# A third group of nodes summed from gathered rows: three of 25 groups in 13 rounds, in place of two in 9

## The chip, the cores and the metric

The kernel runs on one core of one Trainium2 chip. The metric is the device time of one execution in microseconds; where several executions are timed, the median stands for them.

## What is computed

One layer of a graph network on 6250 nodes with 206250 edges, 128 features each, all float32. The edges come sorted by their target node `dst`; `src` is in no order.

```python
def _L0_gnn_ref(node_features, edge_features, src, dst, W_node, b_node, W_edge, b_edge, W_msg, b_msg):
    h = node_features @ W_node.T + b_node
    e = edge_features @ W_edge.T + b_edge
    msg = h[src] + e
    msg = msg @ W_msg.T + b_msg
    n = node_features.shape[0]
    s = jax.ops.segment_sum(msg, dst, num_segments=n)
    deg = jax.ops.segment_sum(jnp.ones(dst.shape, msg.dtype), dst, num_segments=n)
    return s / jnp.maximum(deg, 1.0)[:, None]

x = _layernorm(x + _L0_gnn_ref(x, edge_attr_128, src, dst, ...), axis=-1)
```

## The kernel before

The two products with weights are taken out of the sum over edges: a node needs the sum of the edge features that point at it, the sum of the rows `x[src]` of those edges, and its number of edges. The nodes are cut into 25 groups of 250 (`NB`).

**Edge features.** The edges are cut into 101 blocks of 2048. SP loads a block of 1 MB (line 483) into one of three buffers `edges`; a buffer is free when PE has read the block that was there (`l1_done`). DVE builds a one-hot table (`onehot`, line 923) and a placing table (`place`, line 929). PE sums the block into 32-wide windows with 16 matmuls a quarter of the array wide (line 691), ACT copies them (line 1448), PE places them in 144 columns (line 698) and DVE adds these to `sums_e` (line 944).

**Rows of x, by counts.** For most groups the sum of `x[src]` is made as a product: a matrix of counts (how often node j is a source of target i) by x. A round does this for one group. POOL loads the group's pieces of `src` (`load_window`, line 604); DVE makes keys and then five pairs of one-hot tables `row_hot` and `key_hot` (`make_hots`, line 954), one pair for each of the round's five segments. PE makes the counts in 25 fills of five matmuls, five fills a segment (`count_fill`, line 802); ACT moves each fill out of PSUM (`move_bank`, lines 1539 to 1547); PE multiplies the counts by x in 98 matmuls (`apply_counts`, line 814), spread over the second half of the round and the first of the next. Before there are 23 rounds.

**Rows of x, gathered.** For the remaining `GX` groups, 2 before, the rows are fetched. The first `XBLOCKS` edge blocks, 9, cover the edges of these groups. For each of the 2048 edges of such a block POOL gathers the row `x[src]` into `x_gathered`, by 16 indirect DMAs of 128 rows (`load_rows`, line 625), and PE sums the block a second time with these rows in place of the edge features (line 691 with `x_gathered`), with the same tables, into columns of `sums_e` set aside for it (`X_COLS`, `X_LONG`).

There is one buffer `x_gathered`. The first gather of block k waits until PE has used block k−1, and each gather waits for a fill of the rounds:

```python
room = (x_round[k] - x_round[k - 1] if k > 0 else 2) * ROUND_FILLS
x_fill.append([x_round[k] * ROUND_FILLS + XSEG * FILLS - room + 2 + (room - 9) * i // (TILES - 1) for i in range(TILES)])
...
if k > 0:
    pool.wait_ge(l1_done, last_item[sup_of.index(k - 1)] + 1)
pool.wait_ge(bank_filled, x_fill[k][i])
```

PE uses a gathered block at the start of the round's fourth segment (`XSEG` = 3), behind fill 15 of 25, once all 16 DMAs have landed (`rows_in`). `x_round` says which rounds have one: before 5, 6, 8, 10, 12, 13, 15, 17 and 19. The gathers and the window loads share POOL in the order of their fills (`pool_loads`); a round's window load stands at fill 10. The other edge blocks are taken in pairs, in the third and the fifth segment of each round.

**Finishing.** When a group's sums are whole, PE multiplies them by the weights (`finish_group`, lines 826 and, for a gathered group, 829) into the bank `misc_ps`, which must be free of the group finished before; DVE adds message, bias and residual and takes the statistics, ACT normalises, SP stores. The group of round m is finished in the first segment of round m+2. A gathered group is finished once the blocks that hold it are summed (`X_DONE`).

Of the kernel before, what the change touches and what calls it, by code (L numbers as in the profile page):

```python
# [31 lines left out]
SEGS = 5  # L32
# [10 lines left out]
EDGE_SLOTS = 3  # L43
ONEHOT_SLOTS = 3
COUNT_BANKS = 3
GX = 2
XBLOCKS = 9
X_COLS = 2000
X_LONG = 700
BLOCK = 128  # L50
JOBS = 2
NEAR = 3
# [5 lines left out]
def gnn_layer(nc, x, src, dst, edge_attr, w_node, b_node, w_edge, b_edge, w_msg, b_msg, out):  # L58
# [5 lines left out]
    GROUPS = N // NB  # L64
    ROUNDS = GROUPS - GX
    B_ROUNDS = GROUPS - G0
# [9 lines left out]
    def area_of(b):  # L76
        return max(0, STEP * b - AHEAD)
# [5 lines left out]
    JOB_DVE = (13, 4)  # L83
    JOB_ROWS = (B_ROUNDS - NEAR, G0 - GX)
    JOB_ROUND = (NEAR, B_ROUNDS)
# [13 lines left out]
    SLOTS_B, SLOTS_A, DEGREES = 9, 17, 13  # L99
    group_of = [G0 + m if m < B_ROUNDS else GX + m - B_ROUNDS for m in range(ROUNDS)]  # L100
    XSEG = 3
    x_round = [5 + 14 * k // (XBLOCKS - 1) for k in range(XBLOCKS)]
    x_slot = [LEAD + SEGS * m + XSEG for m in x_round]
    ordered = [FIRST + i if FIRST + i < NS else FIRST + i - NS + XBLOCKS for i in range(NS - XBLOCKS)]
    PAIRS = -(-(NS - XBLOCKS - LEAD) // 2)
    sup_of, blocks_at, ordered_by, items_by, item_of = [], [], [0], [0], []
    for u in range(SLOTS):
        m, s = divmod(u - LEAD, SEGS)
        pairs = -(-PAIRS * (2 * m + (s >= 2) + (s >= 4)) // (2 * ROUNDS))
        due = u + 1 if u < LEAD else min(NS - XBLOCKS, LEAD + 2 * pairs)  # L110
        blocks_at.append(list(range(len(sup_of), len(sup_of) + due - ordered_by[-1])))
# [3 lines left out]
        if u in x_slot:  # L115
            assert not blocks_at[u]
            k = x_slot.index(u)
# [8 lines left out]
    slot_of = [next(u for u in range(SLOTS) if t in blocks_at[u]) for t in range(NS)]  # L126
    assert x_round[-1] < B_ROUNDS + 2 and sorted(sup_of) == list(range(NS)) and max(len(ts) for ts in blocks_at) <= 2 and ITEMS == NS + XBLOCKS


    X_DONE = [5, 9]  # L130
    ordered_x = {u: sum(len(blocks_at[w]) for w in range(u)) for u in range(SLOTS + 1)}
    finishes = [(LEAD + SEGS * (m + 2) + (3 if m == 0 else 0) if m < ROUNDS - 2 else SLOTS, m, None) for m in range(ROUNDS)]
    for i in range(GX):
        u = x_slot[X_DONE[i] - 1] + SEGS
        finishes.append((u if u not in x_slot else u + SEGS, None, i))
    finishes.sort(key=lambda f: f[0])
    finish_slot = [f[0] for f in finishes]
    finish_of = {m: n for n, (u, m, i) in enumerate(finishes) if m is not None}
# [3 lines left out]

    ZERO_FIN = 1 + max(n for n, g in enumerate(finished) if g * NB < X_COLS + X_LONG and (g + 1) * NB > X_COLS)
    ZERO_X = finish_slot[ZERO_FIN - 1] + 1
    assert ZERO_X < x_slot[0] and X_COLS >= N0 + AREA and area_of(XBLOCKS - 1) + AREA <= X_LONG and area_of(SCRATCH_SAFE - 1) + AREA <= SCRATCH

# [3 lines left out]
    for u, m, i in finishes:  # L150
# [3 lines left out]
        if m is None:  # L154
            assert LIMIT_X[0] + LIMIT_X[1] * (2 * i + 1) <= X_DONE[i]
        elif m < B_ROUNDS:
# [15 lines left out]
    with ExitStack() as ctx:  # L172
        def sb(name, shape, dt=F32):
            return ctx.enter_context(nc.sbuf_tensor(name, shape, dt))
# [92 lines left out]
        deg_rows = rows_words[0:CHUNKS, JOBS * (NB + 2) + PB + 1:JOBS * (NB + 2) + 2 * PB + 1]  # L267
        limit_x = sb("limit_x", [2 * GX, 1])
        limit = [sb(f"limit{k}", [JOB_ROWS[k], 1]) for k in range(JOBS)]
# [640 lines left out]
        def _(dve):  # L910
# [249 lines left out]
            def make_degrees():  # L1160
                dve.wait_ge(chunk_rows_in, 32)
                dve.tensor_scalar(check_junk[0:2 * GX, 16:17], chunk_rows[0:2 * GX, PB:PB + 1], limit_x[:, 0:1], None, ALU.is_gt, ALU.add,
                                  accum_out=viol[0:2 * GX, 13:14])
# [274 lines left out]
        def _(act):  # L1438
# [135 lines left out]
            for u in range(SLOTS):  # L1574
# [3 lines left out]
                if u == ZERO_X:  # L1578
                    act.wait_ge(fin_mm, ZERO_FIN)
                    act.copy(sums_e[:, X_COLS:X_COLS + X_LONG], zero_col[:, 0:1].to_broadcast([P, X_LONG])).then_inc(zeroed, 1)  # L1580
                if u < LEAD:
# [84 lines left out]
```

## Time and profile before

| | us |
|---|---|
| median of 3 runs | 718.48 (717.97 to 718.91) |
| the profiled execution | 714.08 |
| span in its profile | 712.2 |
| PE busy | 647.9 |
| DVE busy | 591.8 |
| ACT busy | 460.3 |
| POOL busy | 234.6 |

The span is the time from the first to the last recorded instruction of the profiled execution; 1.9 us lie outside it. PE is the matmul engine, PEld its weight loads, DVE the vector engine, ACT the scalar engine, POOL the one that issues the gathers, SP the one that issues plain loads and stores. "Busy" is time in which an engine has an instruction in work. In a timeline row the first number is the start in us from the span's start, the second the time that the row covers, and the brackets tell the idle time ahead of it and what ended that.

### The profile page before, as it was taken

The numbers are of one execution on the slowest core, as the hardware profiler recorded it, in microseconds if no ns is written. First come the engines' busy times: TensorE is split into PE (matmuls) and PEld (weight loads), VectorE is DVE, ScalarE is ACT, GpSimd is POOL, SyncE is SP. The second block draws the span as 40 slices with busy tenths as digits, with TensorE's granted clock in tenths as the row PEclk, the third lists the DMA queues.
The fourth block names the chain that finished last, engine by engine and source line by source line (L and its number), as shares of the span: only waits on it lengthen the run. The fifth ranks groups of instructions, "written<-read, shape, count | busy, mean of one in ns | idle before, by whom it ended". The sixth has DMA issues, their size and how long they took to land.

```text
span 712.2 us, 22423 instructions
## 1 busy us (share of the span) xinstructions
PE 647.9 (91%) x9313; PEld 592.6 (83%) x9313; DVE 591.8 (83%) x1156; ACT 460.3 (65%) x954; POOL 234.6 (33%) x199
## 2 busy tenths in 40 slices
PE   2699977989999979999999999799999999999994
PEld 2577866878989969999999889798899999989994
DVE  7685697869999868998989899598899898898873
ACT  3147798637657646766767666476677676676772
POOL 3212000210534755434435548354255255000000
PEclk9999999979999999999999999999999999999998
DMA  6881524534556764765865466665755865853400
GB/s 201 288 254 40 168 98 136 186 120 167 185 180 209 254 223 145 263 198 170 279 199 165 153 216 206 213 207 180 233 207 195 260 195 181 274 174 135 143 15 18
DMA packets 81507, 130.55 MB, mean 183 GB/s; under 512 B 12100, under 2 KB 25126, under 8 KB 81303
## 3 DMA queue, kind: packets, MB, share of 16 engines
q1 hardware_dynamic: 73230, 115.79, 48.7%
q0 software_dynamic: 7200, 12.39, 6.2%
q8 instruction: 77, 1.26, 0.7%
q10 hardware_dynamic: 974, 0.90, 0.5%
q14 instruction: 26, 0.21, 0.1%
HBM read 125.80 MB, written 3.23 MB: 181 GB/s over the span
## 4 chain that ended last, share of the span: by engine, by line
PE 75%; DVE 11%; issue 4%; ACT 4%; DMA 3%; POOL 2%; ACTq 0%; DVEq 0%; POOLq 0%
PE x_ps L814 36%; PE count_ps L802 16%; PE win_ps L691 13%; PE win_ps L698 3%; DVE key_hot L954 3%; DVE row_hot L954 2%; PE misc_ps L826 2%; POOL x_gathered L625 1%; DMA x_gathered<-in_x_dram,x_index 1%; PE x_ps L737 1%; DVE x_gathered L1075 1%; PE count_ps L737 1%; ACT counts L1539 1%; DMA win_src<-in_src_dram,clipped_int 1%; PE x_ps L721 1%
## 5 line engine op out<-in xcount | busy, mean ns | idle before, releaser
L814 PE MATMUL x_ps<-x_parts,counts 128*125 128x256 f32 x2254 | 391.2, 301 | 6.5 <-ACT counts L1544 6.5
L1547 ACT CAST counts<-count_ps 128x490 fp32r<-128x490 f32 x552 | 321.9, 604 | 105.3 <-PE count_ps L802 102.5
L814 PEld LDWEIGHTS x_ps<-x_parts,counts 128*125 128x125 f32 x2254 | 299.6, 189 | 9.8 <-ACT counts L1544 9.8
L625 POOL DMA_INDIRECT x_gathered<-in_x_dram,x_index x144 | 186.6, 1296 | 243.8 <-PE count_ps L802 231.0
L954 DVE TENSOR_TENSOR row_hot<-iota_bf,row 125x3200 bf16<-125x3200 bf16 x115 | 209.6, 1822 | 50.9 <-PE count_ps L802 29.3
L802 PE MATMUL count_ps<-key_hot,row_hot 125*128 125x98 bf16 x2875 | 216.5, 209 | 12.8 <-ACT counts L1547 9.4
L802 PEld LDWEIGHTS count_ps<-key_hot,row_hot 125*128 125x128 bf16 x2875 | 149.2, 98 | 44.1 <-issue 11.3
L954 DVE TENSOR_TENSOR key_hot<-iota_bf,key 125x2500 bf16<-125x2500 bf16 x115 | 167.2, 1454 | 0.0
L691 PE MATMUL win_ps<-edges,onehot 128*32 128x128 f32 x3232 | 104.6, 282 | 0.2 <-DVE sums_e L944 0.2
L691 PEld LDWEIGHTS win_ps<-edges,onehot 128*32 128x32 f32 x3232 | 88.1, 113 | 9.1 <-issue 1.4
L1448 ACT COPY win_sb<-win_ps 128x128 f32<-128x128 f32 x110 | 29.0, 267 | 72.5 <-PE win_ps L691 70.8
L604 POOL DMA_INDIRECT win_src<-in_src_dram,clipped_int x23 | 34.3, 1490 | 82.3 <-DVEq L1122 65.0
L944 DVE TENSOR_TENSOR sums_e<-sums_e,win_ps 128x144 f32<-128x144 f32 x110 | 33.0, 300 | 26.7 <-PE win_ps L698 25.3
L923 DVE TENSOR_TENSOR onehot<-iota_bf,rel_col 128x352 f32<-128x352 bf16 x101 | 48.0, 510 | 0.0
L698 PE MATMUL win_ps<-place,win_sb 128*128 128x144 f32 x220 | 37.2, 290 | 1.6 <-ACT win_sb L1448 1.6
L698 PEld LDWEIGHTS win_ps<-place,win_sb 128*128 128x128 f32 x220 | 31.1, 191 | 2.3 <-ACT win_sb L1448 2.2
L929 DVE TENSOR_SCALAR place<-iota_f,pos 128x144 f32<-128x144 f32 x101 | 30.3, 300 | 0.2
L1566 ACT ACTIVATE y<-y,shift,rstd 125x128 f32<-125x128 f32 x50 | 22.4, 509 | 3.6 <-DVE shift L1041 3.6
L653 PE MATMUL x_ps<-ones_bf,region 101*125 101x1 bf16 x48 | 5.5, 245 | 15.4 <-DVE region L1046 15.4
L1539 ACT CAST counts<-count_ps 128x245 fp32r<-128x245 f32 x23 | 9.0, 391 | 15.3 <-PE count_ps L802 15.3
L653 PEld LDWEIGHTS x_ps<-ones_bf,region 101*125 101x125 bf16 x48 | 5.3, 227 | 16.1 <-DVE region L1046 10.8
L826 PE MATMUL misc_ps<-w_both,sums_e 128*125 128x128 f32 x100 | 16.1, 282 | 2.7 <-issue 2.7
(214 smaller groups left out, 417.2 us busy)
## 6 DMA issues: line engine op xcount, KB each, us to landing
edges<-in_edge_attr_dram SPq DMA_DIRECT2D x101, 1024.0 KB, 6.8
resid<-in_x_dram SPq DMA_DIRECT2D x25, 125.0 KB
out_dram<-y SPq DMA_DIRECT2D x25, 125.0 KB
x_gathered<-in_x_dram,x_index POOLq DMA_INDIRECT x144
region<-in_dst_dram ACTq DMA_DIRECT2D x1, 768.0 KB
win_src<-in_src_dram,clipped_int POOLq DMA_INDIRECT x23, 3.6
x_index<-in_src_dram SPq DMA_DIRECT2D x9, 8.0 KB, 5.8
region<-in_L_gnn_W_node_dram SPq DMA_DIRECT2D x1, 64.0 KB
```

The lines of the kernel that those rows point to most:

```text
L604: pool.indirect_dma_start(out=win_src[:, m % 3, :], out_offset=None, in_=src.rearrange("(r e) -> r e", e=WE), in_offset=bass.IndirectOffse ...
L625: pool.indirect_dma_start(out=x_gathered[:, i, :], out_offset=None, in_=x[:, :], in_offset=bass.IndirectOffsetOnAxis(ap=x_index[:, k, i:i ...
L691: mm = pe.matmul(bank[q * W:(q + 1) * W, 0:D], hot[:, q * J + j, :], rows, start=(j == 0), stop=(j == J - 1))
L698: pe.matmul(l2_ps[v % 2], win_sb[:, v % 2, :], place[:, t % 2, :], start=True, stop=True).then_inc(l2_done, 1)
L802: mm = pe.matmul(fill_bank(fill)[:, k * KEYS:(k + 1) * KEYS], row_hot[0:WE, g % 2, f * FILL + k, :], key_hot[0:WE, g % 2, f * FILL + k, 0: ...
L814: mm = pe.matmul(x_ps[m % 2][0:PB, h * 2 * D:(h + 1) * 2 * D], counts[h][:, b, :], x_parts[:, b, :, :].rearrange("p k d -> p (k d)"), star ...
L826: mm = pe.matmul(to, sums_e[:, first + h * PB:first + (h + 1) * PB], w_both[:, 1, :], start=True, stop=(i is None))
L923: dve.tensor_tensor(onehot[:, t % ONEHOT_SLOTS, :, 0:SPAN], iota_bf[:, 0:SPAN].rearrange("p (a w) -> p a w", a=1).to_broadcast([P, TILES, ...
L929: dve.tensor_scalar(place[:, t % 2, :], iota_area[:, :], pos[:, sup_of[t]:sup_of[t] + 1], None, ALU.is_equal).then_inc(place_ready, 1)
L944: dve.tensor_tensor(to, to, l2_ps[v % 2], ALU.add).then_inc(added, 1)
L954: ins = dve.tensor_tensor(hot[0:WE, g % 2, :, :].rearrange("p w (a b) -> p w a b", b=4), iota_bf[0:WE, 0:width].rearrange("p (c a b) -> p ...
L1547: ins = act.copy(counts[h][:, :, at - h * PB:at - h * PB + FILL * 2], nodes)
```

## The change

`GX` goes from 2 to 3 and `XBLOCKS` from 9 to 13. With one group more gathered there are 22 rounds in place of 23. The gathered blocks stand in the rounds 7 to 19, one in each, in place of every second round or so from 5 to 19. The set-aside columns grow from 700 to 950. A gathered group is finished three segments after the segment of its last block, in the second segment of the next round, in place of five or ten after it.

```diff
-GX = 2
-XBLOCKS = 9
+GX = 3
+XBLOCKS = 13
 X_COLS = 2000
-X_LONG = 700
+X_LONG = 950
...
     XSEG = 3
-    x_round = [5 + 14 * k // (XBLOCKS - 1) for k in range(XBLOCKS)]
+    x_round = [7 + k for k in range(XBLOCKS)]
     x_slot = [LEAD + SEGS * m + XSEG for m in x_round]
...
-    X_DONE = [5, 9]
+    X_DONE = [5, 9, 13]
...
     for i in range(GX):
-        u = x_slot[X_DONE[i] - 1] + SEGS
-        finishes.append((u if u not in x_slot else u + SEGS, None, i))
+        finishes.append((x_slot[X_DONE[i] - 1] + SEGS - 2, None, i))
```

The changed file is one line shorter, so that a line behind the diff has a number less by one there.

POOL's program, from the first gathered blocks on. In the kernel before (`win_src` is the window load of a round, `x_gathered` a gather, with how many stand in a row):

```order
L604 DMA win_src<-in_src_dram,clipped_int 125x125 x4
L625 DMA x_gathered<-in_x_dram,x_index 128x128 x7
L604 DMA win_src<-in_src_dram,clipped_int 125x125
L625 DMA x_gathered<-in_x_dram,x_index 128x128 x9
L604 DMA win_src<-in_src_dram,clipped_int 125x125
L625 DMA x_gathered<-in_x_dram,x_index 128x128 x16
L604 DMA win_src<-in_src_dram,clipped_int 125x125
L625 DMA x_gathered<-in_x_dram,x_index 128x128 x7
L604 DMA win_src<-in_src_dram,clipped_int 125x125
L625 DMA x_gathered<-in_x_dram,x_index 128x128 x9
```

The same place in the changed kernel:

```order
L603 DMA win_src<-in_src_dram,clipped_int 125x125 x6
L624 DMA x_gathered<-in_x_dram,x_index 128x128 x7
L603 DMA win_src<-in_src_dram,clipped_int 125x125
L624 DMA x_gathered<-in_x_dram,x_index 128x128 x9
L603 DMA win_src<-in_src_dram,clipped_int 125x125
L624 DMA x_gathered<-in_x_dram,x_index 128x128 x16
L603 DMA win_src<-in_src_dram,clipped_int 125x125
L624 DMA x_gathered<-in_x_dram,x_index 128x128 x16
```

A block with a round between it and the one before has its 16 gathers split by a window load, 7 and 9; a block in the next round has all 16 between two window loads. Before there are two such blocks, now twelve, all but the first.

PE's program around the finish of the first gathered group. Before, in the fourth segment of round 14 (`turn_keys` is lines 786 and 787, then the four matmuls of the finish):

```order
L786 MATMUL misc_ps<-ident_bf,row_bf 125x125
L787 MATMUL misc_ps<-ident_bf,key_bf 125x125
L802 MATMUL count_ps<-key_hot,row_hot 128x98 x5
L814 MATMUL x_ps<-x_parts,counts_49 125x256 x5
L826 MATMUL misc_ps<-w_both,sums_e 125x128
L829 MATMUL misc_ps<-w_both,sums_e 125x128
L826 MATMUL misc_ps<-w_both,sums_e 125x128
L829 MATMUL misc_ps<-w_both,sums_e 125x128
```

In the changed kernel, in the second segment of round 12 and the start of the third (`edges` at the end is the pair of blocks there):

```order
L801 MATMUL count_ps<-key_hot,row_hot 128x98 x5
L813 MATMUL x_ps<-x_parts,counts_50 125x256 x4
L825 MATMUL misc_ps<-w_both,sums_e 125x128
L828 MATMUL misc_ps<-w_both,sums_e 125x128
L825 MATMUL misc_ps<-w_both,sums_e 125x128
L828 MATMUL misc_ps<-w_both,sums_e 125x128
L801 MATMUL count_ps<-key_hot,row_hot 128x98 x5
L813 MATMUL x_ps<-x_parts,counts_50 125x256 x5
L690 MATMUL win_ps<-edges,onehot 32x128 x32
```

The finish of the gathered group now stands ahead of the round's first pair of blocks, five fills behind the finish of the group that is finished in that round's first segment. With three of them, they fall in rounds 12, 16 and 20; before in 14 and 20.

## Rows read from the trace of the kernel before

**Rows 1.** The page: span, busy time and share of engines; index load.
```profile
span 712.2 us, 22423 instructions
PE 647.9 (91%) x9313; PEld 592.6 (83%) x9313; DVE 591.8 (83%) x1156; ACT 460.3 (65%) x954; POOL 234.6 (33%) x199
...
x_index<-in_src_dram SPq DMA_DIRECT2D x9, 8.0 KB, 5.8
```
**Rows 2.** Windows by round: rounds 6, 7, 8, 13, 20, 22; 5 to 22 together.
```profile
243.71:276.61 32.90, 28.70 (x438) 26.34 (x435) 24.15 (x43) 18.40 (x38) 17.71 (x14) 0.95 0.61 199
276.61:301.41 24.80, 24.49 (x370) 22.88 (x367) 22.78 (x39) 17.65 (x36) 14.21 (x11) 1.00 0.61 209
301.41:328.68 27.27, 26.96 (x438) 25.06 (x435) 24.00 (x43) 18.40 (x39) 9.29 (x9) 1.00 0.67 220
...
431.90:464.52 32.62, 28.55 (x438) 26.24 (x435) 24.18 (x43) 18.40 (x39) 17.65 (x14) 0.95 0.62 198
...
623.31:650.81 27.50, 26.06 (x382) 24.29 (x378) 24.08 (x47) 17.91 (x37) 0.00 (x0) 1.00 0.53 178
...
675.17:696.03 20.86, 20.55 (x258) 19.05 (x254) 14.17 (x19) 15.73 (x31) 0.00 (x0) 1.00 0.06 14
...
216.46:696.03 479.57, 462.46 (x7023) 429.88 (x7019) 414.82 (x714) 323.82 (x666) 191.44 (x147) 0.99 0.59 194
```
**Rows 3.** Waits of PE over the span: total us, times, longest us.
```profile
PE win_ps L691 <- DMA x_gathered<-in_x_dram,x_index: 7.6, 2, 3.9
```
**Rows 4.** Timeline of POOL, 234 to 268 us: round 6's block and the next one's start.
```profile
234.03 0.95 POOL L625 DMA_INDIRECT x_gathered<-in_x_dram,x_index  x1 [8.71 <-PE count_ps L802]
235.28 0.94 POOL L625 DMA_INDIRECT x_gathered<-in_x_dram,x_index  x1 [0.30 <-issue]
...
247.15 2.30 POOL L625 DMA_INDIRECT x_gathered<-in_x_dram,x_index  x1 [0.30 <-PE count_ps L802]
...
253.63 2.09 POOL L625 DMA_INDIRECT x_gathered<-in_x_dram,x_index  x1 [0.30 <-issue]
...
257.39 1.00 POOL L625 DMA_INDIRECT x_gathered<-in_x_dram,x_index  x1 [0.30 <-issue]
258.70 2.58 POOL L604 DMA_INDIRECT win_src<-in_src_dram,clipped_int  x1 [0.31 <-issue]
266.93 0.95 POOL L625 DMA_INDIRECT x_gathered<-in_x_dram,x_index  x1 [5.65 <-PE count_ps L802]
```
**Rows 5.** Timeline of POOL, 422 to 456 us: round 13's block, first and last gather.
```profile
422.21 1.17 POOL L625 DMA_INDIRECT x_gathered<-in_x_dram,x_index  x1 [8.80 <-PE count_ps L802]
...
445.56 0.94 POOL L625 DMA_INDIRECT x_gathered<-in_x_dram,x_index  x1 [0.30 <-issue]
...
454.85 0.95 POOL L625 DMA_INDIRECT x_gathered<-in_x_dram,x_index  x1 [5.46 <-PE count_ps L802]
```
**Rows 6.** Timeline of PE: uses of the blocks of rounds 5, 6 and 13.
```profile
230.95 1.06 PE L691 MATMUL win_ps<-x_gathered,onehot 128*32 128x128 f32 x32
...
262.27 1.94 PE L691 MATMUL win_ps<-x_gathered,onehot 128*32 128x128 f32 x32 [3.88 <-DMA x_gathered<-in_x_dram,x_index]
...
450.33 1.94 PE L691 MATMUL win_ps<-x_gathered,onehot 128*32 128x128 f32 x32 [3.76 <-DMA x_gathered<-in_x_dram,x_index]
```
**Rows 7.** Windows of 2 us around the late use in round 6.
```profile
262.00:264.00 2.00, 1.73 (x32) 1.51 (x32) 0.00 (x0) 0.00 (x0) 0.00 (x0) 0.57 0.97 339
...
266.00:268.00 2.00, 2.00 (x24) 1.98 (x24) 1.07 (x4) 1.20 (x2) 0.95 (x1) 1.00 0.04 11
```
**Rows 8.** Timeline of DVE in round 6: two of its tables `row_hot`.
```profile
246.81 1.82 DVE L954 TENSOR_TENSOR row_hot<-iota_bf,row 125x3200 bf16<-125x3200 bf16 x1 [0.45 <-PE count_ps L802]
...
253.08 1.82 DVE L954 TENSOR_TENSOR row_hot<-iota_bf,row 125x3200 bf16<-125x3200 bf16 x1
```
**Rows 9.** Timeline of PE: finish of the first gathered group, round 14.
```profile
482.75 0.46 PE L826 MATMUL misc_ps<-w_both,sums_e 128*125 128x128 f32 x2 [1.12 <-issue]
```

## The prediction

> **What bounds the kernel now.** I read the page first, then the busy times round by round, then the waits of PE, and last the timelines of POOL, PE and DVE around the two longest of those waits. The page says that PE is busy 91% of a 712.2 us span and POOL 33% [rows 1]. By these averages PE bounds the kernel and POOL has room. The rounds correct that. In the windows the first number is a round's length; then come the busy times of PE, PEld, DVE, ACT and POOL, the granted clock of PE and the DMA's share. A round without a gathered block lasts 24.80 us and one with a block 27.27 us, PE busy in all but 0.31 us of each; two rounds with the same number of matmuls (438) last 32.90 and 32.62 us, and PE's busy time falls 4 us short of them [rows 2]. What fills the gap is one line among PE's waits: line 691 waits for the DMA of `x_gathered`, 7.6 us in two waits, the longest 3.9 us [rows 3].
>
> These two rounds are 6 and 13, the only two of the nine whose block follows a block in the round just before; all others have a round between them. POOL's timeline shows why. `x_gathered` is one buffer, so the first of the 16 gathers can start only after the block before has been used. From then on POOL stands still only for the 0.30 us between two gathers, and the 16 run from 234.03 to 257.39 + 1.00 = 258.39 us, 24.36 us [rows 4]; in the second case from 422.21 to 445.56 + 0.94 = 446.50 us, 24.29 us [rows 5]. PE uses the data at 262.27 and 450.33 us, after waits of 3.88 and 3.76 us [rows 6]: 3.88 and 3.83 us after the last gather left POOL. So in such a round POOL is the bound, through a loop of its own: use, first gather, 16 gathers, landing, use.
>
> **The change part by part.** Rounds 0 to 4 hold no gathered block before or after, and the tail behind the last round is the same work; I take both at no change. The sum is thus over rounds 5 to 22, 479.57 us in the profile of before [rows 2].
>
> One round goes: its 125 matmuls of line 802, 98 of line 814, the 25 evictions and the five pairs of one-hot tables. The 101 edge blocks stay, and four of them are used a second time with gathered rows. I don't price these one by one, since whole rounds of each kind stand in the trace.
>
> *Rounds 5 and 6* lose their gathered blocks and become plain: 2 × 24.80 = 49.6 us. *Round 7* holds the first block, whose gathers have two rounds of room: 27.27 us. *Rounds 8 to 19* are the question. All twelve hold a block right behind another, the state that before has twice. The fills that release the gathers come from the same formula with a room of 25, so it is the same program as in rounds 6 and 13. Once each round is like that, the loop is: from the late use to the first gather 266.93 − 262.27 = 4.66 us and 454.85 − 450.33 = 4.52 us [rows 4 to 6]; gathers 24.36 and 24.29 us; landing 3.88 and 3.83 us. Together 32.90 and 32.64 us, which are the lengths of the two rounds themselves. PE does not catch up: each round starts the same loop again. Twelve rounds at the mean of 32.90 and 32.62, 32.76 us, give 393.1 us.
>
> The 4.6 us are longer than in a round that was not late: after the use at 230.95 us the first gather starts at 234.03, 3.08 us later [rows 4, 6]. The difference is PE itself. After its idle wait the granted clock is 0.57 in the stretch from 262 us, half-speed 1.2 GHz for most of it, and back at 1.00, 2.4 GHz, by 266 us [rows 7]; the 32 matmul records take 1.94 us there instead of 1.06 [rows 6]. So one wait costs 32.76 − 27.27 = 5.5 us: some 3.8 of waiting and 1.7 of slow clock.
>
> *Round 20* is plain with two groups to finish, as the last such round of before: 27.50 us. There PE waits 1.12 us ahead of line 826 [rows 9], because the pair of blocks just ahead must be added first. In the second segment no blocks stand ahead, but the finish of the round's own group does, one segment earlier, and its messages must be read from the same bank first; I take the price as it was, bounds 1.1 us less and 3 us more. The other two extra finishes fall in rounds 12 and 16, inside the 3.8 us that PE waits anyway; if that cover went, they would cost some 2.7 us each, the difference of 27.50 and 24.80. *Round 21*, the last, has one edge block: 20.86 us.
>
> Sum: 49.6 + 27.3 + 393.1 + 27.5 + 20.9 = 518.4 us against 479.6: **+38.8 us**. Without the twelve waits it would be 12 × 5.49 = 65.9 us less, 27.1 us under before; the change thus buys 27 us of work and pays 66.
>
> Edits at nothing: the window load on POOL (line 604) stands behind the 16 gathers of its round and ends at 258.70 + 2.58 = 261.28 us, before the use [rows 4]; it would cost its 2.6 us if it came before the last gather. Four more index loads on SP in rounds 0 to 3 lie ahead of edge blocks for which PE never waits; if that reserve is smaller than I think, an index load delays a block by at most its own landing, 5.8 us [rows 1]. The zeroed stretch grows by 250 columns on ACT, which is busy 18.40 of 27.27 us in a round [rows 2].
>
> What could move the twelve rounds. *Below:* if the clock stayed up after a shorter wait, the loop would be 3.08 + 24.3 + 3.9 = 31.3 us, 17.5 us less over twelve rounds. *Above:* the gathers are uneven. An undisturbed one takes 0.94 us and the gap 0.30, but some take 2.30 or 2.09 [rows 4]. Each of these starts while DVE is in `row_hot` and ends 0.82 us after it: 249.45 against 246.81 + 1.82 = 248.63, and 255.72 against 253.08 + 1.82 = 254.90 [rows 4, 8]. One more such hit in each round would be up to 2.30 − 0.94 = 1.36 us, 16.3 us in all. I keep 24.3: since a held gather ends with `row_hot` whenever it began, POOL falls back into the same step each round.
>
> A rule of the Trainium skill weighs on that term. SBUF — State Buffer, section "Who interferes with whom", says that a two-input DVE operation such as `tensor_tensor` contends with GpSimd instructions that read SBUF, not with those that only write it, and infers that writing a DMA's descriptors is untouched by it. By that inference the gathers would not be held, and the time would be that of the first rival below. The trace sides with the first half of the rule: these gathers read their row numbers from `x_index`, and they are held.
>
> **The rivals.** *No wait (faster).* PE reaches the use 27.27 us after the one before. With 3.08 us to the first gather and 3.88 of landing, the 16 gathers have 20.3 us, 1.27 each. Undisturbed they take 16 × (0.94 + 0.30) = 19.8 us, so the wait vanishes if DVE's tables don't hold POOL. Time: 718.48 − 27.1 = 691.4 us. It is what the inference of that page would give. For it: POOL is idle most of the span. Against it: both dense rounds of before were held, for 24.36 and 24.29 us. Chance 0.06.
>
> *A shorter loop.* The wait stays but the clock does not fall, or the landing gets quicker as the collisions with edge loads shift: 31.3 us a round, 718.5 + 21.3 = 739.8 us. For it: in rounds 10, 12 and 16 the work ahead of the use differs. Against it: both waits cost the clock. Chance 0.17.
>
> *A longer loop.* One more gather held a round, 34.1 us: 718.5 + 55.1 = 773.6 us. For it: finishing a group adds DVE operations with two inputs. Against it: the two dense rounds agree within 0.3 us. Chance 0.11.
>
> *The gathers don't move as said.* The program order shows 16 gathers between every two window loads, so nothing is left to this beyond 0.01, at no change.
>
> **How the numbers follow.** The forecast, twelve full waits, has 0.65. Its sum is made against the profiled execution, 714.08 us, and gives 752.9; the median of the runs shown, 718.48, is 4.4 us above that execution, so I add the 38.8 to the median: 757.3 us. Its own range is 748 to 766, from the finishes and half a microsecond a round. The range over all reaches to the shorter and the longer loop, 738 to 774, and leaves out the 0.06 of no wait and the edges. A measurement of this kernel can tell about 0.2% from no change. Slower by more has the forecast, both other loops and no share of the rest: 0.93; faster 0.06; the same 0.01.
>
> **What would show it.** In the changed kernel PE's waits on line 691's successor for the DMA of `x_gathered` should be twelve, some 3 to 4 us each, 40 to 46 us in all; uses in rounds 8 to 19 about 32.8 us apart; the granted clock down after each; POOL with no idle time but 0.30 us between the gathers. Two or fewer such waits, or uses 27.3 us apart, would make the forecast wrong, and uses 31.3 us apart with a clock at 1.00 would make it the shorter loop.

## The result, and the profile after

The changed kernel takes 764.1 us (762.2 to 767.5, 4 runs) against 718.2 us before: 45.9 us more, a ratio of 1.064 (95% interval 1.061 to 1.067). Forecast were 757.3 us, with 738 to 774 as the range and slower as the likely side. The profiled execution has a span of 761.0 us, 48.8 us above that of before.

The page of the changed kernel, with the busy times and the engines' shares of the chain of work that ended last:

```profile
span 761.0 us, 22355 instructions
PE 653.1 (86%) x9228; PEld 594.1 (78%) x9228; DVE 577.3 (76%) x1144; ACT 445.9 (59%) x929; POOL 317.0 (42%) x262
...
PE 46%; POOL 9%; DMA 8%; issue 5%; DVE 2%; ACT 1%; POOLq 0%; DVEq 0%
```

The same chain in the kernel before:

```profile
PE 75%; DVE 11%; issue 4%; ACT 4%; DMA 3%; POOL 2%; ACTq 0%; DVEq 0%; POOLq 0%
```

PE's share of the span falls from 91% to 86% [rows 1], in a kernel that has one round less to compute. On the chain PE falls from 75% to 46%, while POOL goes from 2% to 9% and DMA from 3% to 8%. PE's waits say where (total us, times, longest us):

```profile
PE win_ps L690 <- DMA x_gathered<-in_x_dram,x_index: 52.1, 12, 8.7
```

Two waits of 7.6 us together [rows 3] have become twelve of 52.1 us. The rounds, by windows (length; busy time of PE, PEld, DVE, ACT, POOL; granted clock; DMA share; GB/s), first rounds 5 to 21 together, then rounds 7, 12, 13, 16 and 20:

```profile
214.08:745.19 531.11, 472.05 (x6938) 435.33 (x6934) 401.86 (x704) 309.62 (x641) 287.57 (x221) 0.94 0.56 185
264.02:291.28 27.26, 26.95 (x438) 25.07 (x435) 24.21 (x43) 18.37 (x38) 13.89 (x12) 1.00 0.67 223
424.76:458.66 33.90, 29.84 (x446) 27.50 (x443) 25.99 (x53) 19.11 (x42) 20.98 (x17) 0.95 0.60 195
458.66:492.65 33.99, 29.75 (x438) 27.39 (x435) 24.31 (x43) 18.39 (x39) 22.51 (x17) 0.90 0.62 206
560.93:596.16 35.23, 29.80 (x446) 27.30 (x443) 26.39 (x55) 19.10 (x41) 21.42 (x17) 0.95 0.59 187
697.62:724.30 26.68, 25.77 (x378) 23.88 (x375) 23.70 (x46) 18.22 (x39) 0.00 (x0) 1.00 0.36 122
```

Round 7, whose block has two rounds of room, lasts 27.26 us as its like before. The twelve rounds 8 to 19 run from 291.28 to 697.62 us: 406.3 us, 33.9 each, where the forecast had 393.1. Round 13 has the work of the dense rounds of before [rows 2] and lasts 33.99 us, with a granted clock of 0.90.

One turn of the loop, on PE's timeline (a use and the next one) and on POOL's (first gather, second, a held one, the last, and the window load):

```profile
477.26 1.94 PE L690 MATMUL win_ps<-x_gathered,onehot 128*32 128x128 f32 x32 [3.93 <-DMA x_gathered<-in_x_dram,x_index]
...
511.64 1.93 PE L690 MATMUL win_ps<-x_gathered,onehot 128*32 128x128 f32 x32 [4.32 <-DMA x_gathered<-in_x_dram,x_index]
```

```profile
482.06 0.95 POOL L624 DMA_INDIRECT x_gathered<-in_x_dram,x_index  x1 [5.91 <-PE count_ps L801]
484.20 0.94 POOL L624 DMA_INDIRECT x_gathered<-in_x_dram,x_index  x1 [1.19 <-PE count_ps L801]
...
496.08 2.31 POOL L624 DMA_INDIRECT x_gathered<-in_x_dram,x_index  x1 [0.30 <-PE count_ps L801]
...
506.32 0.94 POOL L624 DMA_INDIRECT x_gathered<-in_x_dram,x_index  x1 [0.30 <-issue]
507.57 2.57 POOL L603 DMA_INDIRECT win_src<-in_src_dram,clipped_int  x1 [0.30 <-issue]
```

From use to first gather 482.06 − 477.26 = 4.80 us, gathers to 506.32 + 0.94 = 507.26, so 25.20, landing 511.64 − 507.26 = 4.38: 34.38 us. Against the loop of before [rows 4 to 6] the gathers and the landing have grown. The second gather shows why the gathers did: POOL stands 1.19 us ahead of it until PE has made a fill, where before it stood 0.30 [rows 4]. PE makes that fill late because its clock stays down longer; windows of 2 us behind the use:

```profile
478.00:480.00 2.00, 2.00 (x31) 1.62 (x24) 0.00 (x0) 0.51 (x2) 0.00 (x0) 0.50 0.57 175
480.00:482.00 2.00, 2.00 (x14) 1.90 (x13) 0.00 (x0) 0.95 (x2) 0.00 (x0) 0.50 0.18 49
482.00:484.00 2.00, 2.00 (x20) 1.97 (x20) 1.10 (x4) 0.58 (x1) 0.95 (x1) 0.77 0.10 33
```

The granted clock is 0.50, 1.2 GHz, to 482 us and part of the stretch behind it, where before it was back at 1.00 four microseconds after the use [rows 6, 7].

### The profile page after: what moved, and what is told of

It reads as the page before. It is cut to its first block, busy times and chain, and to the rows that moved or that the text cites. A ratio compares the mean times of both kernels' runs of the same rounds, so it can differ in the third digit from the quotient of the medians.

```text
span 761.0 us, 22355 instructions
## 1 busy us (share of the span) xinstructions
PE 653.1 (86%) x9228; PEld 594.1 (78%) x9228; DVE 577.3 (76%) x1144; ACT 445.9 (59%) x929; POOL 317.0 (42%) x262
## 3 DMA queue, kind: packets, MB, share of 16 engines
HBM read 129.96 MB, written 3.23 MB: 175 GB/s over the span
## 4 chain that ended last, share of the span: by engine, by line
PE 46%; POOL 9%; DMA 8%; issue 5%; DVE 2%; ACT 1%; POOLq 0%; DVEq 0%
PE x_ps L813 24%; PE count_ps L801 11%; POOL x_gathered L624 9%; DMA x_gathered<-in_x_dram,x_index 8%; PE win_ps L690 8%; PE win_ps L697 2%; PE misc_ps L825 1%; DVE key_hot L953 1%; DVE row_hot L953 0%; DVE onehot L922 0%; DVE y L1004 0%; ACT y L1565 0%; ACT counts L1538 0%; ACT counts L1543 0%; DVE stats L1025 0%
## 5 line engine op out<-in xcount | busy, mean ns | idle before, releaser
L813 PE MATMUL x_ps<-x_parts,counts 128*125 128x256 f32 x2156 | 382.9, 306 | 6.2 <-ACT counts L1543 6.1
L1546 ACT CAST counts<-count_ps 128x490 fp32r<-128x490 f32 x528 | 308.2, 604 | 120.0 <-PE count_ps L801 115.8
L624 POOL DMA_INDIRECT x_gathered<-in_x_dram,x_index x208 | 260.9, 1254 | 184.9 <-PE count_ps L801 151.5
L813 PEld LDWEIGHTS x_ps<-x_parts,counts 128*125 128x125 f32 x2156 | 294.5, 194 | 9.3 <-ACT counts L1543 9.3
L953 DVE TENSOR_TENSOR row_hot<-iota_bf,row 125x3200 bf16<-125x3200 bf16 x110 | 200.3, 1821 | 51.8 <-ACT key L1525 26.6
L801 PE MATMUL count_ps<-key_hot,row_hot 125*128 125x98 bf16 x2750 | 211.1, 212 | 10.7 <-ACT counts L1546 8.5
L953 DVE TENSOR_TENSOR key_hot<-iota_bf,key 125x2500 bf16<-125x2500 bf16 x110 | 159.8, 1453 | 0.0
L603 POOL DMA_INDIRECT win_src<-in_src_dram,clipped_int x22 | 42.4, 1928 | 133.0 <-DVEq L1121 65.6
L690 PE MATMUL win_ps<-x_gathered,onehot 128*32 128x128 f32 x416 | 22.4, 383 | 52.1 <-DMA x_gathered<-in_x_dram,x_index 52.1
L690 PEld LDWEIGHTS win_ps<-x_gathered,onehot 128*32 128x32 f32 x416 | 17.5, 152 | 55.0 <-issue 55.0
L922 DVE TENSOR_TENSOR onehot<-iota_bf,rel_col 128x352 f32<-128x352 bf16 x101 | 48.8, 516 | 0.0
```

Source lines behind the costliest of these rows:

```text
L603: pool.indirect_dma_start(out=win_src[:, m % 3, :], out_offset=None, in_=src.rearrange("(r e) -> r e", e=WE), in_offset=bass.IndirectOffse ...
L624: pool.indirect_dma_start(out=x_gathered[:, i, :], out_offset=None, in_=x[:, :], in_offset=bass.IndirectOffsetOnAxis(ap=x_index[:, k, i:i ...
L690: mm = pe.matmul(bank[q * W:(q + 1) * W, 0:D], hot[:, q * J + j, :], rows, start=(j == 0), stop=(j == J - 1))
L801: mm = pe.matmul(fill_bank(fill)[:, k * KEYS:(k + 1) * KEYS], row_hot[0:WE, g % 2, f * FILL + k, :], key_hot[0:WE, g % 2, f * FILL + k, 0: ...
L813: mm = pe.matmul(x_ps[m % 2][0:PB, h * 2 * D:(h + 1) * 2 * D], counts[h][:, b, :], x_parts[:, b, :, :].rearrange("p k d -> p (k d)"), star ...
L922: dve.tensor_tensor(onehot[:, t % ONEHOT_SLOTS, :, 0:SPAN], iota_bf[:, 0:SPAN].rearrange("p (a w) -> p a w", a=1).to_broadcast([P, TILES, ...
```

## The experiments

The theory is the loop of the prediction: one buffer, so use, first gather, 16 gathers on POOL (some held while DVE makes its tables), landing, next use, in a row. Three rivals could tell the same story: DMA traffic alone, the third group itself, and a POOL queue that is full. The loop has three pieces: the start (from a use to the first gather), the gathers (from the first to the end of the last), and the landing (from there to the next use). Over the twelve late blocks of the changed kernel they have means of 4.42, 24.95 and 4.29 us, 33.66 together, read from POOL's and PE's timelines as above; the means below are made in the same way.

**Fewer gathers.**

```diff
+GATHERS = 12
-... for k in range(XBLOCKS) for i in range(TILES)])
+... for k in range(XBLOCKS) for i in range(GATHERS if k else TILES)])
-                    pe.wait_ge(rows_in, 16 * TILES * (k + 1))
+                    pe.wait_ge(rows_in, 16 * (TILES + GATHERS * k))
```

> The changed kernel with 12 of the 16 gathers of each block from the second block on; the other rows keep what the first block left there, so the sums of the gathered groups are not the reference's. Loop theory (one buffer, POOL issues 16 gathers between two uses, 33.9 us a round where PE needs 27.27): 12 gathers take some 19 us, the loop is 3.1 + 19 + 4 = 26 us, under PE's 27.27, so the twelve waits vanish and the time is 764.1 - 12 x 6.6 = 685 us (683 to 692). Rival, DMA traffic (the rows come late because the DMA engines are full with five blocks of edges a round): a quarter fewer row bytes is 3% of a round's traffic, the waits stay near 4 us, and the time is over 745 us.

Measured: 691.0 us, ratio 0.965 (0.960 to 0.970) to the kernel before. One wait of 2.4 us is left of twelve, and round 14 is at PE's own length; behind it stands the same round of the changed kernel:

```profile
PE win_ps L691 <- DMA x_gathered<-in_x_dram,x_index: 2.4, 1, 2.4
```

```profile
459.22:486.47 27.25, 26.94 (x437) 25.06 (x435) 23.99 (x43) 18.39 (x39) 15.72 (x13) 1.00 0.73 241
```

```profile
492.65:526.63 33.98, 29.34 (x432) 26.98 (x429) 23.91 (x43) 18.14 (x38) 22.11 (x17) 0.90 0.59 191
```

The DMA engines are busier in the shorter round, 0.73 and 241 GB/s against 0.59 and 191. So the traffic of five edge blocks and three quarters of a block of rows fits; the run with more places, below, shows the same with the whole block. What does not fit is 16 gathers between two uses.

**The placement alone.** Two groups, nine blocks, in nine rounds in a row:

```diff
-    x_round = [5 + 14 * k // (XBLOCKS - 1) for k in range(XBLOCKS)]
+    x_round = [7 + k for k in range(XBLOCKS)]
...
-        u = x_slot[X_DONE[i] - 1] + SEGS
-        finishes.append((u if u not in x_slot else u + SEGS, None, i))
+        finishes.append((x_slot[X_DONE[i] - 1] + SEGS - 2, None, i))
```

> The kernel before, two groups and nine blocks in 23 rounds, with its blocks in nine consecutive rounds (7 to 15) and each group finished in the second segment of the next round. Loop theory: eight waits in place of two, rounds 8 to 15 at 33.9 us: 718.2 + 8 x 33.9 + 27.3 - 7 x 27.3 - 65.5 = about 760 us (752 to 764), although no group is moved. Rival, the third group costs (four more blocks, 4 MB more rows, four more index loads): within 3 us of 718.

Measured: 755.2 us, ratio 1.054 (1.050 to 1.057). Eight waits stand on PE:

```profile
PE win_ps L690 <- DMA x_gathered<-in_x_dram,x_index: 35.8, 8, 8.6
```

The loss comes with the placement (and the earlier finish, which by itself costs nothing, as the next run shows), at the work of the kernel before. The third group is not what costs.

**The finish alone.** The last two lines of the diff above on the kernel before, with its own rounds.

> The kernel before with the finish of its two gathered groups in the second segment of the round behind their last block, nothing else. By the changed kernel's round 20 (26.68 us in place of 27.50) each finish gives 0.8 us, and the first one falls into round 13, whose PE waits for rows anyway: 2.7 us. Together 3.5 us, 0.5%, faster. Rival, the bank is not yet free from the finish one segment earlier: no gain or slower.

Measured: 715.0 us, ratio 0.997 (0.993 to 1.000). The interval holds both no change and the gain of 0.5% that was expected, so the median can't tell them apart; the profiled executions have spans of 712.3 us and 712.2 before. The windows show where a gain goes (rounds 13, 14 and 20 of this run, then round 14 of before):

```profile
432.77:467.72 34.95, 30.71 (x446) 28.20 (x443) 25.98 (x53) 19.09 (x41) 16.28 (x14) 0.90 0.57 189
467.72:492.52 24.80, 24.49 (x370) 22.87 (x367) 23.15 (x39) 17.64 (x36) 13.50 (x11) 1.00 0.65 217
624.01:650.67 26.66, 25.75 (x378) 23.85 (x375) 24.77 (x49) 18.23 (x39) 0.00 (x0) 1.00 0.46 157
```

```profile
464.52:492.03 27.51, 26.07 (x382) 24.30 (x378) 24.14 (x47) 17.93 (x38) 14.44 (x11) 1.00 0.62 205
```

Round 14 loses the 2.7 us of the finish and round 20 0.84 us (26.66 against 27.50 [rows 2]), but round 13, where the finish was to hide in the wait, grows from 32.62 to 34.95 us. Three rows of that round (the use of its pair of edge blocks, the last gather, the use of the rows), and the pair's use in the kernel before:

```profile
442.06 1.95 PE L690 MATMUL win_ps<-edges,onehot 128*32 128x128 f32 x64
446.44 0.94 POOL L624 DMA_INDIRECT x_gathered<-in_x_dram,x_index  x1 [0.30 <-issue]
452.46 1.94 PE L690 MATMUL win_ps<-x_gathered,onehot 128*32 128x128 f32 x32 [3.47 <-DMA x_gathered<-in_x_dram,x_index]
```

```profile
439.64 1.95 PE L691 MATMUL win_ps<-edges,onehot 128*32 128x128 f32 x64
```

The finish moves the pair back by 2.4 us and the last gather by only 0.9 (445.56 before [rows 5]). The loads that the pair releases thus come closer to the last gather, and the rows landed 5.1 us after it in place of 3.8. The granted clock of the round was 0.90 in place of 0.95, and the part of the round behind the use took 1.1 us more.

**An earlier start.**

```diff
-... - room + 2 + (room - 9) * i // (TILES - 1) for i in range(TILES)])
+... - room + (room - 9) * i // (TILES - 1) for i in range(TILES)])
```

> The changed kernel with the gathers released two fills earlier, so that the first starts as soon as the block before is used. Loop theory: the piece from use to first gather, 4.8 us after a wait, falls to some 2.9 us, and the gathers no longer stand for fills (0.8 us a round): 2 to 2.7 us a round less, 764.1 - 12 x 2.3 = 736 us (730 to 742). Rival, DMA traffic: the landing takes up what the start gives, 760 us or more.

Measured: 741.4 us, ratio 1.034 (1.031 to 1.037), as expected. The pieces are 2.37, 24.56 and 4.84 us. The start falls by 2.0 us, the gathers by 0.4, and the landing takes back 0.5. Twelve waits are left:

```profile
PE win_ps L690 <- DMA x_gathered<-in_x_dram,x_index: 36.7, 12, 7.6
```

**DVE's tables made small.** From round 5 on each table is made for one target in place of 25.

```diff
+                n = BATCH if m < 5 else 1
-                    shape = [WE, BATCH, width // 4, 4]
+                    shape = [WE, n, width // 4, 4]
-                    ins = dve.tensor_tensor(hot[0:WE, g % 2, :, :]...
+                    ins = dve.tensor_tensor(hot[0:WE, g % 2, 0:n, :]...
-                                            four[0:WE, m % 2, s * BATCH:(s + 1) * BATCH, :]...
+                                            four[0:WE, m % 2, s * BATCH:s * BATCH + n, :]...
```

> The changed kernel with DVE's two one-hot tables of a segment made for one target in place of 25 from round 5 on; PE goes on with the tables of the rounds before, so counts are wrong and PE's work is the same. If DVE's tables hold POOL (held gathers end 0.82 us after row_hot): no gather over 1.3 us, 16 of them in 20 us in place of 25, loop 27 to 28.5 us, waits under 1.5 us, time 690 to 705 us. Rival, the long gathers come from POOL's own queue being full: four long gathers a block stay, and the time is over 755 us.

Measured: 709.9 us, ratio 0.991 (0.987 to 0.995), 5 us over the expected band. All gathers of the run, and of the changed kernel (count: least, median and greatest duration in ns):

```profile
L624 POOL DMA_INDIRECT x_gathered<-in_x_dram,x_index x208: 938/944/1145, 233.2 to 626.3; - x104
```

```profile
L624 POOL DMA_INDIRECT x_gathered<-in_x_dram,x_index x208: 940/1058/2597, 230.0 to 677.9; - x104
```

Not one long gather is left of 208: it is DVE's work on these tables that holds them, not a queue of POOL's own. The gathers fall to 20.53 us a block, but the landing grows to 5.47, so that eleven waits stay, 19.6 us in all, and a turn takes 29.24 us. In the stretch from the last gather to the use in round 14 the DMA engines have no room left (share 1.03), and the pair of edge blocks is used some 3 us ahead of the last gather's end, where in the changed kernel it is 6.9:

```profile
482.18:487.90 5.72, 3.57 (x62) 3.02 (x61) 2.11 (x8) 3.25 (x8) 1.22 (x2) 1.00 1.03 362
```

The next run tries behind what the rows stand.

**Half the edges.** From round 5 on SP loads half of each edge block.

```diff
+                n = Q if slot_of[t] < LEAD + SEGS * 5 else 2
-                sp.dma_start(edges[:, t % EDGE_SLOTS, :, :]...q=Q), edge_rows[...]...
+                sp.dma_start(edges[:, t % EDGE_SLOTS, 0:n * J, :]...q=n), edge_rows[...]...[:, 0:n, :])...
```

> The changed kernel in which SP loads half of each edge block (512 KB of 1 MB) from round 5 on, the other half keeping the rows of blocks before, so the edge sums are wrong and PE's work is the same. If the landing, 4.3 us in the mean, is spent behind edge loads in the DMA engines: landing about 2 us, a round 31.3 us in place of 33.9, 764.1 - 12 x 2.5 = 734 us (728 to 745), the gathers on POOL unchanged at 24 to 25 us. Rival, the landing is the gather's own latency: landing stays over 3.8 us and the time over 757 us.

Measured: 723.3 us, ratio 1.009 (1.006 to 1.012), 5 us better than the expected band. The mean landing is 2.27 us, half of 4.29, while the gathers take 24.73 us as before. One turn, the last gather and the use:

```profile
613.73 0.95 POOL L625 DMA_INDIRECT x_gathered<-in_x_dram,x_index  x1 [0.30 <-issue]
```

```profile
616.93 1.08 PE L691 MATMUL win_ps<-x_gathered,onehot 128*32 128x128 f32 x32 [2.19 <-DMA x_gathered<-in_x_dram,x_index]
```

The same stretch, from the last gather to the use, in the changed kernel and in this one:

```profile
507.26:511.64 4.38, 0.06 (x4) 0.03 (x1) 3.16 (x3) 0.27 (x1) 2.58 (x2) 0.84 1.04 379
```

```profile
614.68:616.93 2.25, 0.06 (x5) 0.04 (x2) 2.25 (x3) 0.27 (x1) 1.95 (x1) 1.00 0.53 109
```

The DMA share there falls from 1.04 to 0.53. So about half of the landing is time behind edge blocks; in round 11 alone it stays at 4.37 us. DMA traffic is not the bound by itself, but it sizes this piece of the loop. At eleven of the twelve waits the use took 1.08 us, not 1.94: the clock stayed up, which gives the rest of the gain, 3.33 us to the first gather in place of 4.42.

**PE busy while it waits.** Sixteen matmuls on constants stand ahead of each wait; nobody reads their results.

```diff
+                    for d in range(16 if k > 0 else 0):
+                        pe.matmul(bank[:, D:2 * D], ident[:, :], ones[:, :], start=True, stop=True)
                     pe.wait_ge(rows_in, 16 * TILES * (k + 1))
```

> The changed kernel with 16 matmuls more on PE, on constants into columns that nobody reads, just ahead of the wait for the rows of each block from the second on: some 3.5 us of work in place of idle time. If the slow clock after each wait lengthens the loop: the granted clock stays at 1.00, the first gather comes 3.1 us after the use in place of 4.8, the gathers no longer stand for fills (0.8 us), and a round falls from 33.9 to 31.5 us: 764.1 - 12 x 2.4 = 735 us, although PE does more. Rival, the wait alone counts and the clock is hidden in it: 762 us or more.

Measured: 747.3 us, ratio 1.044 (1.040 to 1.048): 17 us less than the changed kernel where 29 were expected, with 3.8 us more work on PE in each of twelve rounds.

```profile
341.44 3.84 PE L687 MATMUL win_ps<-ones,ident 128*128 128x128 f32 x32
346.31 1.08 PE L692 MATMUL win_ps<-x_gathered,onehot 128*32 128x128 f32 x32 [1.04 <-DMA x_gathered<-in_x_dram,x_index]
```

```profile
346.00:348.00 2.00, 1.69 (x41) 1.49 (x41) 0.00 (x0) 0.51 (x2) 0.00 (x0) 1.00 0.74 233
```

The clock is at 1.00 behind the use. The pieces are 3.23, 24.47 and 4.48 us: start and gathers return to nearly what they are after a use in time, and a turn is 1.5 us shorter. That is the clock's part of the loop, or the least of it: eight waits are left, and in the other four blocks the added work ends behind the landing and delays the use. The landing, which I had put at 3.9, is not helped. About 4 us of the miss lie ahead of round 8, in rounds that the edit does not touch.

**More places for rows.** Twelve more tiles of 128 rows, eleven of them in buffers that are free after round 4 and one new, so that gathers can go ahead of the use:

```diff
+        x_tiles = [x_gathered[:, i, :] for i in range(TILES)] + ([rows_words[:, i * D:(i + 1) * D] for i in range(7)] + ...)[0:12]
...
-                    if k > 0:
-                        pool.wait_ge(l1_done, last_item[sup_of.index(k - 1)] + 1)
+                n = TILES * k + i
+                if n >= len(x_tiles):
+                    pool.wait_ge(l1_done, last_item[sup_of.index((n - len(x_tiles)) // TILES)] + 1)
...
-... - room + 2 + (room - 9) * i // (TILES - 1) for i in range(TILES)])
+... - room + 2 + (room - 9) * i // (TILES - 1) - (12 if k > 0 else 0) for i in range(TILES)])
```

Two semaphores in turn count the arrivals, one for every second block, and the first gather into the new places waits for `viol_ready` besides.

> The changed kernel with 28 places for gathered rows in place of 16 (twelve more of 128 rows, in memory that is free after round 4), so that up to 12 gathers of a block go ahead of the use of the block before; they are released 12 fills earlier. All 16 gathers of all blocks stay. Loop theory: POOL needs 24 to 25 us for 16 gathers and 1.3 to 2.6 us for the window load, 25.5 to 27.5 us a round against PE's 27.27, and no longer stands still from the last gather to the next use, so the waits vanish or stay under 1 us: 686 to 698 us. Rival, DMA traffic at the time of the use: waits near 4 us stay, over 740 us.

Measured: 692.7 us, ratio 0.967 (0.963 to 0.970) to the kernel before: faster than both kernels. One wait is left:

```profile
PE win_ps L695 <- DMA x_gathered<-in_x_dram,x_index: 2.9, 1, 2.9
```

A stretch of one round's length in the middle shows PE at its own pace and POOL at 22 of 27 us:

```profile
459.00:486.30 27.30, 26.99 (x435) 25.10 (x435) 24.19 (x43) 18.43 (x39) 22.12 (x18) 1.00 0.72 246
```

With four places more instead of twelve (`[0:4]`, released four fills earlier):

> The changed kernel with 20 places for gathered rows, four more, released four fills earlier. Loop theory: four gathers go ahead of the use, 12 follow it: 3.1 + 18.5 + 4.3 = 25.9 us, under PE's 27.27, so the waits vanish with these as with twelve places more: 690 to 698 us. Rival, POOL's total of 25.5 to 27.5 us a round is the bound, and only a deep stock of gathers hides its uneven steps: waits of 1 to 2 us a round, 710 us or more.

Measured: 700.2 us, ratio 0.977 (0.972 to 0.982), nearer to the theory than to the rival (710 us or more), but 2 us over the theory's band. Four waits are left:

```profile
PE win_ps L695 <- DMA x_gathered<-in_x_dram,x_index: 4.0, 3, 2.7
...
PE win_ps L695 <- DMA rows_words<-in_x_dram,x_index: 2.7, 1, 2.7
```

And the twelve places in the kernel before:

> The kernel before (two groups, nine blocks) with the same twelve places more. Loop theory: its two waits vanish, 2 x 5.5 us: 706 to 708 us. Rival, the places or the earlier release disturb other transfers: 717 us or more.

Measured: 708.0 us, ratio 0.987 (0.983 to 0.991), as expected. Between the two kernels with twelve places more, two groups and three, lie 15.3 us (708.0 − 692.7; each has one wait left): that is what the third group gives by itself.

## Why the prediction was right, and what it mis-sized

**The bound.** Right. The twelve waits are there, on the line named, and twelve rounds are of the kind that stood twice in the profile of before. Two of the signs came out otherwise: the waits are 52.1 us in place of 40 to 46, from 1.7 to 8.7 us each, and POOL does not stand still for 0.30 us alone. Fewer gathers (691.0 us) and more places (692.7) take them away, and the placement alone (755.2) brings them without the third group.

**The size of the twelve rounds.** Mis-sized: 393.1 us forecast, 406.3 measured, 1.1 us a round. This one term is the miss: rounds 5 to 21 take 531.1 us against the 518.4 of the sum. (Rounds 0 to 4 ended 2.4 us earlier than before, 214.08 against 216.46 us, so that the spans differ by 48.8 us; by medians it is 45.9, 7.1 above the forecast's 38.8.) The mean turn of 33.66 us holds the first one, 31.2 us, whose block before was used in time. The other eleven take 33.88 us: a start of 4.54, put at 4.6; gathers of 25.00, put at 24.3; a landing of 4.34, put at 3.9.

The step that failed is that both dense rounds of before stood alone, with a prompt use ahead: I took their gathers as those of a chain of late ones. In the chain the clock is often still down when the first gathers are released. In seven of the twelve blocks POOL stands 0.81 to 1.34 us ahead of the second gather until PE has made a fill, 0.5 us a turn; with PE kept busy none of these stands is left, and the gathers are back at 24.47 us. The landing's excess is explained in part only. In rounds 12 and 16 the finish brings the pair of edge blocks 1.5 and 1.1 us closer to the last gather, and the rows land after 4.90 and 5.82 us; why they take 4.4 to 5.0 us in rounds 9, 14, 17 and 18, where the pair stands as it stood before, is open.

**"POOL falls back into the same step each round."** Borne out: four held gathers in eleven of the twelve blocks, five in round 11. The row said that a held gather ends 0.82 us after `row_hot`; the run with small tables has none above 1.145 us. This is also the verdict on the rule of the Trainium skill (SBUF — State Buffer, "Who interferes with whom"): its contention between two-input DVE operations and GpSimd instructions that read SBUF fits what is seen here; its inference that writing a DMA's descriptors is untouched does not hold for these indexed gathers.

**The cover of the finishes.** Wrong in part. I let the finishes in rounds 12 and 16 vanish in the wait. Round 16 lasted 35.23 us, 1.4 over the mean of 33.9, round 12 33.90. The run of the finish alone shows one way: it delays blocks, these delay loads, and the rows land later. In round 16 the fourth held gather also took 2.55 us, where 2.08 to 2.10 is usual. Round 20, put at 27.50 us, took 26.68: without the blocks just ahead the finish costs 0.8 us less.

**The clock's part.** I had 1.7 us of slow clock in each wait's 5.5; a busy PE gave back 1.5 a turn, or more. Not every round shows it alike.

**The work bought.** The forecast says that the change buys 27 us of work and pays 66. These 27 us hold the two waits that the kernel before also has, 2 × 5.5 us. By the forecast's own rows the work alone is 16 us; the two kernels with more places differ by 15.3.

**The rivals.** No wait: its time, 691.4 us, is what the kernel comes to when the loop is cut (692.7), but it takes more places or fewer gathers; DVE's tables alone, which the rival made its condition, leave 709.9 us, because the landing is then 5.47 us and not the rival's 3.88. The shorter loop (739.8) is about what an earlier start gives, 741.4, though not by the rival's way. The longer loop (34.1 us a round, 773.6) is nearer in size to the 33.9 us measured than the forecast's 32.76, but its mechanism, one more held gather in each round, stands in round 11 alone. In time the forecast is the nearer of the two (757.3 and 773.6 against 764.1), in part because the medians differ by 2.9 us less than the profiled spans: that much is luck.

Round 11 made PE wait 8.7 us, although its turn took 33.7 us as the others: PE came early. It was ready again 25.05 us after the use in round 10 (376.04 to 401.09 us), where a round at its own pace takes 27.27. Round 10 lacks the second pair of edge blocks, and its use is the one late use behind which the clock stayed at 1.00. Left open: why the block of round 10 landed in 1.8 us after its last gather, with its pair of blocks as far ahead as in the others.

## What to carry to other kernels

A unit that is busy a third of the span (POOL, 33% before) can still be the bound, if one buffer ties its work into a loop with its user: add up the loop (release, issue, landing, use) and hold it against the user's own period before more work is put on it. When a profile shows two rounds of the kind that a change will make the rule, their length is the best price there is, but in a chain each round starts from the late state of the one before, and here that cost 1.1 us more a round. Twelve more tiles of buffer, eleven of them in memory that was free by then, turned a change that lost 6% into one that gains 3%; 1.3% of that they give the kernel before as well.

## What was not expected of the hardware

In the kernel before the granted clock was down for 3.4 us at each of the two late uses (262 to 266 us [rows 7]). In the changed kernel it fell at eleven of the twelve late uses, read in windows of 0.5 us: for 3.4 us at three of them, for 6.8 at seven, and for 10.2 at the one after the wait of 8.7 us. Why it stays down longer in the chain is not shown.

Rows that are issued sooner win less than their lead. With small tables the last gather left POOL 5.6 us sooner after the use than in the changed kernel, and the rows landed 4.4 us sooner, because the landing grew from 4.29 to 5.47 us; with half the edge bytes it was 2.27.
